# Attention scores: two stacked fp32r products of 128 rows per head replaced by one plain fp32 product of 64 rows per head, the two heads in the two row halves of the array

## The reference

```
q, k, v = einsum('bsx,xMnd->Mbnsd', x, qkv)
a = q @ k.T * 64 ** -0.5
bias = where(i >= j, cumsum(rpe_bias)[clip(i - j)], -30000)
a = softmax(a + bias);  mix = a @ v
x = layernorm(x + einsum('bnsd,ndx->bsx', mix, out_w))
x = layernorm(x + sigmoid(xr @ W_r.T) * (square(relu(xk @ W_k.T)) @ W_v.T))
```

## Time and profile before

| | |
|---|---|
| median of 3 runs | 1190.78 us (1186.85 to 1191.3) |
| profiled execution, its time | 1187.66 us |
| its span from first to last instruction | 1185.9 us |
| TensorE busy (matmul records, their drain included) | 1115.7 us, 94% |
| VectorE busy | 811.5 us, 68% |
| ScalarE busy | 727.4 us, 61% |
| granted TensorE clock, mean share of full speed | 0.992 |
| transfers, share of 16 DMA engines in queue q1 | 59.5% |

### The profile page before, as it was taken

The page is one execution under the profiler, slowest core; times in us unless marked ns, Lnnn a source line. Parts: engine busy times, 40 slices in busy tenths (PEclk is TensorE's granted clock), DMA queues, the critical chain, the costliest instruction groups (busy, mean ns, idle before and its releaser), DMA issues.

```text
span 1185.9 us, 21563 instructions
## 1 busy us (share of the span) xinstructions
PE 1115.7 (94%) x6973; PEld 783.3 (66%) x6973; DVE 811.5 (68%) x2121; ACT 727.4 (61%) x1857; POOL 6.4 (1%) x15
## 2 busy tenths in 40 slices
PE   5999999989999999999999999999999999999994
PEld 3666666666666667666667666676666667767673
DVE  2666666666667677767677767677767677777756
ACT  3666666666666666666566656566656666656632
POOL 1000000000000000000000000000000000000000
PEclk9999999999999999999999999999999999999997
DMA  8865556565655666656657655657665657665610
GB/s 213 215 150 140 136 137 150 136 177 145 154 150 142 158 153 173 160 143 161 157 150 180 159 145 141 151 150 202 155 149 139 150 153 180 155 154 136 223 55 20
DMA packets 113005, 180.71 MB, mean 152 GB/s; under 512 B 13152, under 2 KB 69360, under 8 KB 112896
## 3 DMA queue, kind: packets, MB, share of 16 engines
q1 hardware_dynamic: 110736, 178.42, 59.5%
q10 hardware_dynamic: 2160, 0.92, 0.3%
HBM read 58.41 MB, written 20.22 MB: 66 GB/s over the span
## 4 chain that ended last, share of the span: by engine, by line
PE 82%; DVE 8%; ACT 5%; issue 4%; DMA 1%; DVEq 0%; SPq 0%; POOL 0%; ACTq 0%
PE ps_o L992 22%; PE ps_t L968 21%; PE ps_rows L954 18%; PE ps_m L929 9%; PE ps_m L934 5%; PE ps_m L1006 4%; DVE pt L667 3%; DVE prob L643 3%; ACT prob L486 3%; PE ps_rows L1062 1%; DMA prob<-in_L_attn_x 1%; ACT pt L504 1%; PE ps_t L973 1%; DVE mix_sb L674 1%; ACT xk_t L522 1%
## 5 line engine op out<-in xcount | busy, mean ns | idle before, releaser
L486 ACT ACTIVATE prob<-prob,low 128x128 f32<-128x128 f32 (+7 forms) x512 | 394.6, 772 | 129.4 <-DVE low L643 125.1
L643 DVE CUSTOM_DVE_ANT_0 prob<-ps_rows,table 128x128 f32<-128x128 f32 (+7 forms) x512 | 378.8, 748 | 56.2 <-PE ps_rows L954 55.4
L954 PE MATMUL ps_rows<-stacks 128*128 128x512 f32 (+3 forms) x1536 | 401.9, 372 | 6.3 <-issue 4.4
L968 PE MATMUL ps_t<-ident,prob 128*128 128x128 f32 x2304 | 347.2, 277 | 30.7 <-DVE pt L667 23.1
L968 PEld LDWEIGHTS ps_t<-ident,prob 128*128 128x128 f32 x2304 | 261.0, 140 | 134.7 <-issue 96.2
L667 DVE COPY pt<-ps_t 128x512 f32<-128x512 f32 (+3 forms) x352 | 200.4, 577 | 178.8 <-PE ps_t L968 176.9
L992 PE MATMUL ps_o<-pt,v_pair 128*64 128x512 f32 (+3 forms) x1536 | 268.6, 492 | 0.0
L954 PEld LDWEIGHTS ps_rows<-stacks 128*128 128x128 f32 x1536 | 246.0, 190 | 27.1 <-issue 4.6
L504 ACT ACTIVATE pt<-ps_t 128x512 f32<-128x512 f32 (+3 forms) x416 | 187.2, 466 | 114.6 <-PE ps_t L968 114.3
L992 PEld LDWEIGHTS ps_o<-pt,v_pair 128*64 128x64 f32 x1536 | 101.8, 136 | 181.7 <-issue 172.3
L929 PE MATMUL ps_m<-x_cur,w_cur 128*128 128x512 f32 x250 | 130.8, 605 | 2.5 <-issue 1.6
(11 more groups left out here) (114 smaller groups left out, 475.2 us busy)
## 6 DMA issues: line engine op xcount, KB each, us to landing
stacks<-k_hi SPq DMA_DIRECT2D x126, 256.0 KB, 4.5
stacks<-k_lo SPq DMA_DIRECT2D x126, 256.0 KB, 4.9
inv_all<-inverse_sums SPq DMA_DIRECT2D x128, 128.0 KB, 3.3
stacks<-q_hi SPq DMA_DIRECT2D x63, 256.0 KB, 3.8
stacks<-q_lo SPq DMA_DIRECT2D x63, 256.0 KB, 4.3
mix_transposed<-mix_sb SPq DMA_DIRECT2D x62, 256.0 KB, 2.3
table<-bias_by_distance SPq DMA_DIRECT2D x64, 192.0 KB, 3.6
mix_tile<-mix_transposed SPq DMA_DIRECT2D x24, 512.0 KB, 5.3
```

Source lines behind the costliest of these rows:

```text
L486: nc.scalar.activation(row, row, ACT.Exp, bias=low[:, r:r + 1], scale=-1.0, accum_out=total[:, r:r + 1]).then_inc(s_exp, 1)
L643: nc.vector.tensor_tensor_reduce(prob[:, r % PSLOTS, 0:width], ps_rows[:, score_at(r):score_at(r) + width], table[n % 2][:, h, 0:width][:, ...
L954: ins = nc.tensor.matmul(ps_rows[:, at + c0:at + c1], q_st(h, n)[:, P * i:P * i + P], k_st(h, n, low_part)[:, c0:c1], start=(low_part == 0 ...
L968: ins = nc.tensor.transpose(ps_t[k % 2][:, P * b:P * b + P], prob[:, r % PSLOTS, at:at + P], ident[:, :])
```

## The change

Scores are one fp32 product per head and stretch, from 64 rows: head 0 of the pair in partitions 0 to 63 of `q_t`/`k_t`, head 1 in partitions 64 to 127, issued one after the other for each stretch of 512 columns. ACT's copy of the projection (with its scale) is all that stands between the projection and the scores. The rounded copies, the subtraction on DVE, the stacks and their transfers are gone, and `q_t`, `k_t` are double buffered. The rows are ordered by query tile, the two heads next to each other. PE issues the scores of two rows in every even slot. x transposed stays in SBUF for all batches. Slots of the projections, the far mix, the gate and the inverse sums move, and the copies out of `ps_t` alternate between DVE and ACT. `mix_last` gets its own memory. The DVE gate reciprocal moves ahead of the bank copies of slot 11.

```diff
-ROWS = [(h, i) for g in range(TILES // GROUP) for h in range(2) for i in range(GROUP * g, GROUP * g + GROUP)]
+ROWS = [(h, i) for i in range(TILES) for h in range(2)]
@@ def score_at(r):
     if r < NROWS // 2:
         return BANK * (r % 4)
-    width = P * (ROWS[r][1] + 1)
-    return SEQ * (r % 2) + ((SEQ - width) // 2 if width - BANK < SHORTEST else 0)
+    return SEQ * (r % 2)
@@
-EVACUATOR = "010110010100010101110111"
+EVACUATOR = "010110010101010101010101"
-PROJ_SLOTS = (2, 3, 5, 7, 10, 14)
+PROJ_SLOTS = (3, 5, 7, 9, 13, 15)
-LATE_SLOT = 8
-RK_PROJ, GATE = 9, 11
+RK_PROJ, GATE = 10, 11
-MIX_FAR = (2, 5)
+MIX_FAR = (1, 5)
-INV_READY = (4, 13)
-INV_BANK = (5, 21)
+INV_READY = (4, 12)
+INV_BANK = (5, 19)
@@
-        x_cur = sb("x_cur", [P, SEQ])
+        x_cur = sb("x_cur", [P, BATCH, SEQ])
-        q_hi, q_lo, k_hi, k_lo = (sb(n, [P, SEQ], F32R) for n in ("q_hi", "q_lo", "k_hi", "k_lo"))
-        stacks = [sb(f"stacks{a}", [P, 6, SEQ], F32R) for a in range(2)]
+        q_t = [sb(f"q_t{a}", [P, SEQ]) for a in range(2)]
+        k_t = [sb(f"k_t{a}", [P, SEQ]) for a in range(2)]
@@ sync, step: all stack_q, stack_k and load_x_transposed, and their waits, are removed
@@ scalar, project
-                if c == 0 and m > 0:
-                    if m == 1:
-                        act.wait_ge(s_first, 96)
-                    for h in range(2):
-                        act.wait_ge(s_stack[h], 96 * m)
-                    nc.scalar.activation(dst[:, half], proj_bank(m, c), ACT.Copy, scale=scale).then_inc(s_hi, 1)
+                    nc.scalar.activation(dst[m % 2][:, half], proj_bank(m, c), ACT.Copy, scale=scale).then_inc(s_qk, 1)
@@ vector: project (scalar_tensor_tensor of hi and lo) is removed; step
                 for slot in range(NROWS):
-                    if slot == LATE_SLOT:
-                        empty_banks(n, slot)
                     for row in rows_ahead(n, more, slot):
                         bias(*row)
+                    if tile_too and slot == GATE:
+                        tile_step(n, slot)
                     if slot in INV_READY:
                         invert(n, INV_READY.index(slot))
-                    if more and slot in PROJ_SLOTS[:4]:
-                        project(n + 1, PROJ_SLOTS.index(slot))
-                    if slot != LATE_SLOT:
-                        empty_banks(n, slot)
+                    empty_banks(n, slot)
@@ tensor, score(n, r): now for the two rows r and r + 1
-                pe.wait_ge(s_biased, NROWS * n + r + 3 - rows_since(r))
-                    for low_part in range(2):
-                        ins = nc.tensor.matmul(ps_rows[:, at + c0:at + c1], q_st(h, n)[:, P * i:P * i + P],
-                                               k_st(h, n, low_part)[:, c0:c1], start=(low_part == 0),
-                                               stop=(low_part == 1))
+                pe.wait_ge(s_biased, NROWS * n + max(r + h + 3 - rows_since(r + h) for h in range(2)))
+                width = P * (i + 1)
+                for c0 in range(0, width, BANK):
+                    c1 = min(c0 + BANK, width)
+                    for h in range(2):
+                        at = score_at(r + h)
+                        ins = nc.tensor.matmul(ps_rows[:, at + c0:at + c1], q_t[n % 2][head(h), P * i:P * i + P],
+                                               k_t[n % 2][head(h), c0:c1], start=True, stop=True)
+                        if c1 == width:
+                            ins.then_inc(s_score, 1)
@@ tensor, step
-                    for row in rows_ahead(n, more, slot):
-                        score(*row)
+                    if slot % 2 == 0:
+                        for row in rows_ahead(n, more, slot):
+                            score(*row)
```

More of the change, by code:

```diff
@@ L19 @@
 BANK = 512
-SHORTEST = 256
 MASKED = 30000.0
@@ L156, in build @@
         rstd = sb("rstd", [P, 2])
-        mix_last = [stacks[0][:, k, :].bitcast(F32) for k in range(6)] + [table[0][:, 0, :]]
-        x_last = x_cur[:, :].rearrange("p (t c) -> p t c", c=C)
+        mix_last = sb("mix_last", [P, PAIRS - 1, SEQ])
+        x_last = x_cur[:, 0, :].rearrange("p (t c) -> p t c", c=C)
         y1_l, x1_l, shr_l, shk_l, xr_l, xk_l, gate_l, k_l = (prob[:, k, :] for k in range(8))
@@ L248, in chunk_of, with head @@
             return (c % 2, c // 2) if m == 0 else (c // 2, c % 2)
[L250 to L256, removed]
+        def head(h):
+            return slice(D * h, D * h + D)
         def columns(w):
@@ L304, in _ @@
             load_table(0)
[L305 to L312, removed]
             def load_weights(m):
@@ L456, in copy_x @@
                 act.wait_ge(s_setup_t, b + 2)
-                nc.scalar.activation(x_t[b - 1], ps_s[0], ACT.Copy).then_inc(s_xt, 1)
+                nc.scalar.activation(x_cur[:, b, :], ps_s[0], ACT.Copy).then_inc(s_xt, 1)
             def project(m, c):
-                if c == 0 and m > 0:
-                    if m == 1:
-                        act.wait_ge(s_first, 96)
-                    for h in range(2):
-                        act.wait_ge(s_stack[h], 96 * m)
                 act.wait_ge(s_proj, NPROJ * m + c + 1)
@@ L524, in _ @@
             act.wait_ge(s_setup_t, 2)
-            nc.scalar.activation(x_cur[:, SEQ // 2:], ps_s[0][:, SEQ // 2:], ACT.Copy).then_inc(s_x, 16)
+            nc.scalar.activation(x_cur[:, 0, SEQ // 2:], ps_s[0][:, SEQ // 2:], ACT.Copy).then_inc(s_x, 1)
             project(0, 0)
@@ L725, in tile_step @@
                                             ALU.subtract, ALU.mult).then_inc(s_chain, 1)
-            for c in range(4):
-                project(0, c)
             for r in range(LEAD):
@@ L758, in step @@
                         store_mix(n, 0)
-                    if tile_too:
+                    if tile_too and slot != GATE:
                         tile_step(n, slot)
@@ L928, in project @@
                     which, at = chunk_of(m, c)
-                    ins = nc.tensor.matmul(proj_bank(m, c), w_cur[m % 2][:, which, :], x_cur[:, 512 * at:512 * at + 512],
+                    ins = nc.tensor.matmul(proj_bank(m, c), w_cur[m % 2][:, which, :], x_cur[:, m // PAIRS, 512 * at:512 * at + 512],
                                            start=True, stop=True)
@@ L1000, in tile_step @@
                     wait_chunk(n + 1, sum(at <= slot for at in PROJ_SLOTS) - 1)
+                if n == PAIR_STEPS - 1 and slot == OUT_PROJ:
+                    pe.wait_ge(s_v, 2 * PAIR_STEPS)
                 if slot in TILE_MATMULS:
@@ L1027, in _ @@
             pe.wait_ge(s_xt, BATCH - 1)
-            pe.wait_ge(s_lo, 4)
-            for r in range(LEAD):
+            pe.wait_ge(s_qk, 4)
+            for r in range(0, LEAD, 2):
                 score(0, r)
```

101 lines of the change are left out of this document (23 added, 78 removed).

## The result

The kernel after takes 1332.8 us (median of 4 runs), the kernel before 1191.0: a ratio of 1.121, 95% interval 1.118 to 1.124. The forecast said slower, 1231 with a range to 1265; the slowdown is 142 us, not 40. The profiled execution takes 1331.4 us, its span is 1329.7. The kernel before ran at 1187.1 to 1189.9 us beside the experiments; each ratio is to those runs.

The account below looks back on a forecast made before the run. PE was taken to bound the kernel: +32 us of PE work, +16 of waits, -4 and -2 at the start make +42 on 1187.66, 1230, and 1 for the median: 1231; 8-in-10 range 1160 to 1265.

Parts of the forecast that it names:

- Row halves overlap: PE's scores: both heads run at once, 7.7 us a step against 8.7, a gain of 1.0 by columns.
- The rival without overlap: PE's scores run one head after the other, 15.5 us a step; 1415 us in all, chance 0.15.
- An excursion costs 0.25 us: Each of eight score groups a step enters and leaves the half-array form on PE: 2.0 us a step.
- 4.11 against 3.86: Around the old kernel's mix: 4.11 us measured against 3.86 of slots, so entering and leaving cost 0.25 together.
- the sign of free changes: A 1024-column score group taking 1.72 us, not 1.97, between its neighbouring transposes would show that changing form is free.
- The rival with free changes of form: Row halves overlap and entering or leaving the half-array form costs nothing: 64 us less, 1167, chance 0.24.
- the one with loops that don't bind: Rival: DVE reaches its biases earlier than walked through, excursions as forecast: 1178, chance 0.13.
- Three loops of 1.5, 0.95 and 0.5 us: PE waits for DVE's biases before scores at slots 8, 10 and 4: 3.0 us a step together.
- Slots 10 to 12 hold a mix ...: no loop binds there: Scores of slot 10 to those of slot 12: the mix on PE covers DVE's work, so no wait.
- The other slots were moved with their producers: nothing: Moved parts other than the gate's reciprocal were priced at no cost.
- The waits of the kernel before, 2.7 and 2.4 us: PE's estimated waits per period, 2.7 us without tile work and 2.4 with it.
- The waits of today go: The old kernel's PE waits for bank copies vanish in the new order; net waits change +0.3 or +0.6 us, 16 us.

Follow-up runs that it names:

- e3: Kernel after plus a full-array transpose of a constant between the two stretches of each wide pair of scores, four a step: 1388.5 us.
- e4: Kernel after plus the same transposes of a constant as e3, but ahead of the first stretch of each wide pair: 1359.4 us.
- e9: e6 with each head's scores as two fp32r products over all 128 rows, leaving out head separation and low parts: 1168.4 us.
- e6: Kernel after with reciprocals at slot 13, biases in pairs, v read first, ACT taking both banks of the first row of slots 8 and 10: 1216.6 us.
- e2: Kernel after with DVE doing both biases of a row pair together in the even slot, ahead of the bank copies: 1312.2 us.
- e5: Kernel after with DVE's read of the v projection moved ahead of reciprocals, bank copy and mix scaling in slot 12: 1291.2 us.
- e7: Kernel before, old scores one row per slot, with the kernel after's row order, slots, bank engines, gate and reciprocals: 1401.8 us.
- e11: e7 with q and k projected at slots 2, 3, 5, 7 and the reciprocals, v read and banks of e6: 1342.7 us.
- e10: e6 with scores as three fp32r products of 64 rows, low x low left out, subtractions back on DVE, no stacks: 1183.3 us.

## Why the prediction was right in direction and wrong in size

- *Row halves overlap*: right, from the column pairs of the earlier trace rows; the two heads' matmuls start together and pairs of 512 columns 0.43 us apart. The rival without overlap (1415) is dead.
- *An excursion costs 0.25 us*: too small. The 4.11 against 3.86 ends at the first transpose, and more is lost just behind it. The runs show 0.35, and 0.26 behind a wait (e3, e4), so eight cost 2.5 us a step and not 2.0. A group of 1024 columns takes 1.92 us from its first score to the work behind it (654.86 to 656.78), where 1.72 was named as the sign of free changes. Less the 1.0 of columns the form costs 1.5 (e9 against e6), 48 us and not 32. The rival with free changes of form falls with it, and the one with loops that don't bind with e2. In part the loss is seen in the trace: behind the group at 654.86 the first product of the tile work (656.78) has its weights loaded at the same moment and not 0.11 us ahead, and the next starts 0.21 us behind it, not 0.11.
- *Three loops of 1.5, 0.95 and 0.5 us*: right in place and in sum. Before the scores PE is idle 1.44, 0.27 and 0.74 us, each with 0.16 more of wait; that is 2.9 us where 3.0 were forecast. The one of slot 10 is shorter by the wait for a bank copy ahead of it.
- *"Slots 10 to 12 hold a mix ...: no loop binds there"* is the step that failed. The loop behind slot 10 doesn't end at the next scores but at the V chunk of slot 13, by way of `ps_m`, and DVE's queue up to it (two biases of 1024, the gate reciprocal, the reciprocals moved to slot 12, three copies, `store_mix`, the read) outlasts PE's mix. I added up the DVE queue for three stretches and let the mix cover the fourth without adding. Its wait of 1.67 + 0.16 in 23 steps is 42 us. e5 takes it away and gains 42, the 8 us of the clock among them, less the bank copy's wait that came.
- *"The other slots were moved with their producers: nothing"* failed with it. The V chunk was moved to slot 13, right behind the read of slot 12 that it waits for, and this was priced at nothing without a reason.
- *The waits of the kernel before, 2.7 and 2.4 us*, were got by taking an estimate of PE's work from the period, and are too large: idle time is 1.4 and 1.0 us there, with the 0.16 for each wait about 2.1 and 1.5. *"The waits of today go"* was too kind besides: bank copies behind the wide biases took their place (0.41 in slot 9, 0.30 without tile work in slot 12). Together waits grew by about 1.5 us in 8 steps and 3.6 in 23, some 95 us, where 16 were forecast.
- *The gate's reciprocal at nothing*: not tested. It is 0.95 us of the fourth loop, but it stood ahead of the v read in the kernel before as well; only its place against the copy of slot 11 changed.
- *Transfers, double buffers, start*: right as far as the traces show it. The chain has DMA at 1% before and after, so no transfer was in PE's way in the steady part; no run changes the traffic alone. The first transpose of inverse sums comes at 34.4 us, 4.6 earlier, where 6 were forecast.
- The clock wasn't in the sum at all: five steps at 1.6 us, 8 us.

## What to carry to other kernels

A product with half the rows in each half of the array is no free gain against one with full rows and fewer passes: count the columns, and 0.35 us for each time the array goes into the half form and comes out (0.26 behind a wait), and put such products together. When an order of rows changes, add up every engine's queue between each producer and each wait of the busiest engine, through all PSUM banks that it shares, also where a long piece of work seems to cover it. Look also at the transfers that stay: a new order can read what they bring earlier than they bring it, as e7 and e11 do with the stacks.

## What the runs showed of the hardware

- fp32 products of 64 rows in the two row halves overlap fully, as do fp32r ones: two heads of 768 columns each, 1.29 us of columns, stand 1.49 us before the next work (645.24 to 646.73); fp32r pairs of 512 columns start 0.23 us apart (e10).
- Going from full-array products to half-row ones and back costs 0.35 us (e3 against the kernel after), and 0.26 where a wait hides the way in.
- Behind an idle stretch of 1.67 us the granted clock was at 1.2 GHz for most of 3.5 us in 5 of 23 steps, and the step took 42.06 us and not 40.44; behind the same stretch in the other steps it stayed at full speed. In e5, which has no such stretch, no step in this part is long.
- Three fp32r products in row halves (0.23 us a pair) are cheaper than one fp32 product (0.86 a pair) for the same 512 columns: e10, with its subtractions on DVE, is 33 us under e6.
